# Context 0 loaded ahead of x tile 1, its column sum taken before the first x tile's transposes

## What is computed

```python
def fake_quant(x, s, z):
    q = jnp.clip(jnp.round(x / s + z), 0.0, 255.0)
    return (q - z) * s

# attention part: both factors are quantised to bytes
q1 = fake_quant(layernorm(x), x1_scale, x1_zp)
q2 = fake_quant(ctx_4096, x2_scale, x2_zp)
x = x + jnp.matmul(q1, q2)

# feed-forward part, on y = layernorm(x)
gate_logits = jnp.einsum('bsd,ed->bse', y, gate_w)          # 8 experts
weights, selected = jax.lax.top_k(gate_logits, 2)
weights = jax.nn.softmax(weights, axis=2)
result = jnp.einsum('bsd,od->bso', y, base_w) + base_b
low = jnp.einsum('bsd,erd->ebsr', y, lora_A)                # rank 16
x = x + result + 2.0 * jnp.einsum('ebsr,eor,bse->bso', low, lora_B, w_full)
```

## Time and profile before

| | us |
|---|---|
| median of 3 runs | 167.87 (167.79 to 167.91) |
| span of the profiled execution, first to last instruction | 166.1 |
| TensorE busy | 159.7 (96%) |
| VectorE busy | 111.5 (67%) |
| ScalarE busy | 83.8 (50%) |
| GpSimd busy | 29.3 (18%) |

### The profile page before, as it was taken

One profiled execution on the slowest core, in us unless ns is written; L12 is line 12 of the kernel. 1 busy time (PEld: TensorE's weight loads), 2 busy tenths in 40 slices (PEclk: granted clock), 3 DMA queues, 4 the chain that ended last, 5 costly groups with the idle time before them and its releaser, 6 DMA issues.

```text
span 166.1 us, 2372 instructions
## 1 busy us (share of the span) xinstructions
PE 159.7 (96%) x824; PEld 121.6 (73%) x824; DVE 111.5 (67%) x258; ACT 83.8 (50%) x111; POOL 29.3 (18%) x65
## 2 busy tenths in 40 slices
PE   5979999999999999999999999999999999999993
PEld 2334444788888878888878688888788888998882
DVE  3976699999999899995785828881380367122051
ACT  3099869957895644273344097175190719200030
POOL 3702042000500402404630040120052000000000
PEclk9999999999999999999999999999999999999999
DMA  5999999979999699204999955959409995000033
GB/s 203 316 417 419 409 409 361 272 238 318 342 230 266 207 197 358 112 0 79 201 161 197 152 117 103 316 157 134 99 5 194 180 249 193 4 0 2 0 126 126
DMA packets 22045, 32.68 MB, mean 197 GB/s; under 512 B 13714, under 2 KB 13970, under 8 KB 22034
## 3 DMA queue, kind: packets, MB, share of 16 engines
q1 hardware_dynamic: 20016, 25.20, 48.1%
q0 software_dynamic: 2016, 7.34, 24.1%
q10 hardware_dynamic: 2, 0.00, 0.0%
HBM read 22.05 MB, written 4.19 MB: 158 GB/s over the span
## 4 chain that ended last, share of the span: by engine, by line
PE 84%; DMA 7%; SPq 3%; ACT 2%; DVE 2%; issue 1%
PE ps_odd L1134 27%; PE ps_even L1134 20%; PE ps_att L1079 11%; DMA ring<-in_ctx 7%; PE ps_g L1115 5%; PE ps_even L1079 2%; PE ps_g L1118 2%; PE ps_t L1058 2%; PE ps_even L1167 2%; PE ps_even L1168 2%; PE ps_even L1169 2%; ACT qc L460 1%; PE ps_odd L1197 1%; PE ps_odd L1196 1%; PE ps_odd L1195 1%; SPq L266 1%
## 5 line engine op out<-in xcount | busy, mean ns | idle before, releaser
L1134 PE MATMUL ps_odd<-w_hi,yt 128*128 128x512 f32 x128 | 38.0, 406 | 0.0
L1079 PE MATMUL ps_att<-c,c1t 128*128 128x512 f16 x96 | 31.3, 383 | 0.5 <-DVE c L735 0.4
L1134 PEld LDWEIGHTS ps_odd<-w_hi,yt 128*128 128x128 f32 x128 | 23.6, 189 | 5.0 <-issue 0.4
L1134 PE MATMUL ps_even<-w_hi,yt 128*128 128x512 f32 x96 | 26.9, 397 | 0.0
L1115 PE MATMUL ps_g<-ag,yt 128*128 128x272 f32 x64 | 21.6, 372 | 0.0
L1134 PEld LDWEIGHTS ps_even<-w_hi,yt 128*128 128x128 f32 x96 | 17.8, 188 | 3.9
L1134 PE MATMUL ps_odd<-w_lo,yt 128*128 128x512 f32 x64 | 19.6, 392 | 0.0
L1134 PE MATMUL ps_even<-w_lo,yt 128*128 128x512 f32 x48 | 15.1, 403 | 0.0
L746 DVE SCALAR_TENSOR_TENSOR x_sb<-ps_att,q_ss,x_sb 128x512 f32<-128x512 f32 x12 | 8.5, 743 | 9.2 <-PE ps_att L1079 8.6
L541 ACT ACTIVATE y_words<-yt_planes 128x1024 uint16<-128x1024 uint16 x8 | 10.3, 1355 | 8.7 <-DMA yt_planes<-y_planes 8.7
L460 ACT ACTIVATE qc<-ring,q_in,q_rec 128x1024 uint16<-128x1024 f32 x11 | 13.6, 1233 | 1.7 <-DMA ring<-in_ctx 1.3
(11 more groups left out here) (150 smaller groups left out, 300.3 us busy)
## 6 DMA issues: line engine op xcount, KB each, us to landing
ring<-in_ctx SPq DMA_DIRECT2D x12, 512.0 KB, 6.7
x_sb<-in_x SPq DMA_DIRECT2D x8, 512.0 KB, 6.6
w_raw<-in_w_t SPq DMA_DIRECT2D x8, 512.0 KB, 16.1
x_sb<-in_base_b POOLq DMA_DIRECT2D x8, 512.0 KB, 7.7
out_x<-x_sb SPq DMA_DIRECT2D x15, 256.0 KB, 2.4
x_sb<-zfix POOLq DMA_DIRECT2D x6, 512.0 KB, 6.5
x_sb<-in_ctx SPq DMA_DIRECT2D x4, 512.0 KB, 8.4
ag_raw<-in_ag_t SPq DMA_DIRECT2D x1, 544.0 KB, 15.1
```

Source lines behind the costliest of these rows:

```text
L1079: ins = pe.matmul(att_bank(t)[h][:, :], c1t[:, t % 4, k, :], c2[:, k, h * HALF:(h + 1) * HALF], start=(k == 0), stop=(k == CT - 1))
L1134: pe.matmul(ffn_bank[t % 2][h][:, :], rows_of(part, t, k), w[:, k, h * HALF:(h + 1) * HALF], start=start, stop=False)
```

## The change

The change touches the lists of four engines; no function is new, and `keep_warm` goes.

- SyncE: context 0 is asked for ahead of x tile 1.
- GpSimd: `x_scale(0)` stands ahead of `quant_constants`.
- VectorE: behind the statistics of x tile 0 come the memset for tile 2, the cut of context 0, the shift of tile 0 and its two quantised halves, one behind the other; then the statistics of tile 1, the two takes of tile 0, and the shift of tile 1.
- TensorE: nine warm-ups in place of twelve and three; the column sum of context 0 ahead of the transposes of tile 0's first half; three warm-ups behind the transposes of the second half; the transposes of tile 1 behind both products of tile 0 with context 0.

```diff
             load_x(0)
+            load_context(0)
             load_x(1)
-            load_context(0)
             load_x(2)
...
             scale_product()
             square_constants()
+            x_scale(0)
             quant_constants()
-            for k in range(0, 4):
+            for k in range(1, 4):
                 x_scale(k)
...
             variance(0, 0)
-            variance(0, 1)
+            byte_ones(2)
+            cut_context(0)
             x_shift(0)
             quantise_first(0)
-            byte_ones(2)
+            quantise_first(1)
+            variance(0, 1)
+            take_first(0)
+            take_first(1)
             x_shift(1)
-            take_first(0)
-            cut_context(0)
-            quantise_first(1)
             variance(0, 2)
             cut_context(1)
-            take_first(1)
             scale_context(2)
...
-            warm_up(12)
-            keep_warm()
+            warm_up(9)
+            column_sums_first(0)
             transpose_first(0)
-            column_sums_first(0)
             transpose_first(1)
+            warm_up(3)
             attention(0, 0, 0)
+            attention(0, 0, 1)
             transpose_c1(1)
-            attention(0, 0, 1)
             attention(0, 1, 0)
```

More of the change, by code:

```diff
@@ L1026, in warm_up @@
                 for _i in range(n):
[L1027 to L1032, removed]
                     pe.matmul(ps_g[:, :], ones[:, :], ones[:, :].unsqueeze(1).broadcast_to([P, HALF // P, P]),
```

## The result

| | before | changed |
|---|---|---|
| executions first timed, us | 167.28 to 167.91, median 167.79 | 168.96, 169.20, 170.85, 170.85, 172.09 |
| span of the profiled execution, us | 166.1 | 168.9 |
| mean granted clock of the changed executions, in the same order | | 1.0, 1.0, 0.988, 0.990, 0.978 |
| ratio of the comparison | | 1.012, interval 1.0088 to 1.0151 |
| later, side by side (17 and 5 executions): median, us | 167.79 | 170.70, ratio 1.0178 (1.0152 to 1.0204) |

The change makes the kernel slower. The times stand in groups: near 169.1 where the clock stayed up, 1.7 us above it where TensorE ran at half its clock for a stretch.

What follows compares the result with a forecast made beforehand. TensorE, busy without a gap from tile 2's attention at 23.08 us, was taken to set the end. Late x tile 1 moves that start to 24.25, +1.2 us: 167.87 + 1.2 = 169.05, say 169.1; own range 168.7 to 169.5, overall 168.0 to 170.5.

Steps and rivals of the forecast that it cites:

- The bound: TensorE from tile 2's attention at 23.08 us: busy 140.12 of 140.12 us, so any later start delays the end equally.
- The landing by place: DMA queue: landing goes by place, not tensor; context 0, second, lands at 5.4 us, x tile 1, third, at 8.0.
- the rival of the slow context 0: DMA queue: slow transfer goes with context 0, landing 1.3 us later at 6.7; +2.5 us, 170.3; chance 0.08.
- The replay: Steps before tile 2's attention: tile 1's shift at 11.02 us, 2.8 later; second context's attention at 14.12, 1.55 late.
- The sum: Tile 2's attention on TensorE: starts at 24.25 instead of 23.08 us, +1.2 us there and at the end.
- The clock: Rival: TensorE, idling before 14.12 us, falls back to 1.2 GHz; +2.4 us, 170.3, at most 171.5; chance 0.08.
- the three idle stretches: TensorE idle 0.7 us before the first attention, 1.7 until tile 1's transposes at 12.5, 1.0 until 14.1.
- Hidden: Rival: existing TensorE waits before tile 2's attention swallow the delay; no change, 167.9 us; chance 0.13.
- a gain: Rival: loads behind the first three land up to 1.3 us sooner, 0.4 us gained, 167.5; chance 0.07.

Runs made afterwards that it cites:

- the two tries: Kernel before with one TensorE product moved ahead of tile 2's first products, then with three products moved into waits: ratio 0.9995, then 1.0004.
- the swap alone: Kernel before with only the loads of context 0 and x tile 1 exchanged: 168.89 to 170.51 us, ratio 1.0127.
- The two orders of ScalarE: Changed kernel, TensorE's idle time filled, ScalarE scaling context 1 before x tile 1, then also context 3 before taking tile 1's transposes: 169.49, then 168.72 us.
- the filled kernel: Changed kernel with 14 more unused products of ones where TensorE idled: median 169.36 us, ratio 1.0103.

## Why the prediction was right, and where it was not

**The bound.** Right in its main point: what is late at tile 2's attention is late at the end, 2.80 us in both places. It holds for a delay and not for less work: "nothing behind it has idle time" came from a busy time of 140.12 of 140.12, and once products were moved out of TensorE's way, waits of 0.32 and 0.21 us stood there (24.16 to 24.48, 28.80 to 29.01), for ScalarE and for VectorE, which arrive there almost together with TensorE. A gain of the whole chain, those engines' part with it, was not tried.

**The landing by place.** Right: 4.0 us for the second and 6.4 for the third, with the tensors exchanged. The third place is the loose one: 6.4 us from issue to landing in both first profiles, 5.5 and 6.6 in the profiles of the two tries, so it lands between 7.1 and 8.2. x tile 1's statistics start at 8.28 behind the quantising and hide that; the rival of the slow context 0 did not happen.

**The replay.** Right to 0.11 us in every step from tile 0's shift up to 14.05, with ScalarE's wait at 4.60 us. In one step that is luck: the cut came 0.16 early, but the shift had to wait for GpSimd, whose scale for it ended at 7.07 (the chain, 6.24 + 0.83), where the prediction had GpSimd as no wait. So an earlier context 0 gained nothing; 0.4 us had been allowed for it. What makes tile 1 late is, as the prediction had it, VectorE's order, with the landing just hidden behind; the swap alone showed that the third place would have been enough too. The two orders of ScalarE showed that its queue carries the cost.

**The sum.** +1.2 to tile 2's attention was forecast, 24.21 - 23.08 = 1.13 measured with the stretches filled. At the end the filled kernel is 1.68 us (169.36 - 167.68) above the kernel before on the same chip, more than the sum. One reason can be read: the profiled execution of before, on which the sum stands, has a span of 166.1, and its spans on that chip had a median of 165.7; those of the filled kernel are 167.1 to 167.3. A forecast made from one profile inherits where that execution lies among its like. The other 0.2 us lie outside the span: in three of the six filled executions 2.4 to 2.8 us stand around it, in the other three and in the kernel before 1.8 to 2.0; why is open.

**The clock.** This is the step that failed: not its mechanism and not its place, but its chance. The prediction named the three idle stretches to within 0.1 us, gave a fall 0.08, and eight of ten executions had one. By its own sign, matmuls of 0.43 us pitch behind 10 us, it was wrong there: the two matmuls from 15.13 are followed by the next at 15.98, 0.425 us each. That the idle stretches are the cause is shown on the two chips where kernels of both kinds ran: with the longest stretch filled, none of 21 executions had a fall, with the stretches left, 7 of 12.

The chance was taken from one row: at the end of the kernel before, the clock fell 2.0 us after the last matmul, and each stretch here is shorter. That row tells of one idle stretch behind dense work; here three followed one another within 5 us with little between them, and only "two follow one another" stood against it. Its price was taken as half of 2.3 us, from 4.7 us at half clock where the stretches measure 3.41; measured, 25.88 - 24.21 = 1.67 where the stretch at half clock lay over work, 0.95 (25.16 - 24.21) where it began in idle time. At 170.3 the rival was thus near to 170.7 and 170.85, the medians that were measured, and with the chance that the runs give it, it would have been the forecast.

**Hidden, and a gain.** Neither happened; the second context's attention would have had to start by 13.2 for the one, ahead of 12.57 for the other.

## What to carry to other kernels

Before a load is moved up and an engine's order fitted to it, follow what both push back: here tile 1 was ready 2.65 us later (10.91 against 8.26), it had two steps in a strictly ordered engine, and every context behind it paid. When a replay shows that TensorE will idle several times in a row, the fallen clock is a case to be weighed as heavily as the wait itself, and unused products in the idle time are a cheap test of it. And a busy time of 100% on an engine with modelled ends does not show that its waits are gone: compare the pitch of its instructions with what a free run of them takes.

## What the runs showed of the hardware

Four profiles hold five stretches at a granted clock of 0.50 (1.2 GHz) ahead of tile 2's attention; each measures 3.41 us, also where TensorE idles for part of it (2.91 us busy from 12.62). The same kernel met it at 14.71 in one execution and at 12.62 in another, with TensorE, VectorE and ScalarE in the same place to 0.1 us from 7.1 us up to the earlier of the two, so that its price differed by 0.7 us between them. The landing of the third of a series of equal loads varied from 5.5 to 6.6 us between executions, that of the second hardly (4.0 to 4.3).
